# Moving the patch-projection tiles in the attention turns, and spreading the expert weight preparation over three units

## The reference

```python
h = patches(x) @ W + b                       # 768 -> 192 per token
a = layernorm(h)                             # attention, 12 heads of 16
q, k, v = heads(a @ Wq.T), heads(a @ Wk.T), heads(a @ Wv.T); rope(q), rope(k)
w = where(causal, erf(q @ k.T / 4) + 1, 0);  y = (w @ v) / max(sum(w), 1e-6)
h = h + y @ Wproj.T
n = layernorm(h)                             # mixture of experts
top-2 of 8 experts by softmax(n @ Wr), capacity 3920 tokens each, best weights first
routed = scatter_add(weight * (silu(d @ w1) * (d @ w3)) @ w2)     # inner width 768
shared = (silu(n @ s1) * (n @ s3)) @ s2
h = h + routed + shared
```

## Time and profile before

| | |
|---|---|
| median of three runs | 3525.04 us |
| profiled execution | 3521.11 us |
| its span | 3519.2 us |
| PE busy | 3201.1 us (91%) |
| DVE busy | 2435.4 us (69%) |
| ACT busy | 1557.7 us (44%) |
| POOL busy | 1389.7 us (39%) |
| mean granted PE clock | 0.914 of full |

### The profile page before, as it was taken

One profiled execution on the slowest core, in us unless ns is written; L12 is line 12 of the kernel. 1 busy time (PEld: TensorE's weight loads), 2 busy tenths in 40 slices (PEclk: granted clock), 3 DMA queues, 4 the chain that ended last, 5 costly groups with the idle time before them and its releaser, 6 DMA issues. The chain is left out here.

```text
span 3519.2 us, 71932 instructions
## 1 busy us (share of the span) xinstructions
PE 3201.1 (91%) x26164; PEld 2149.2 (61%) x26164; DVE 2435.4 (69%) x4832; ACT 1557.7 (44%) x3223; POOL 1389.7 (39%) x1170
## 2 busy tenths in 40 slices
PE   6999999999999999998229999989999999999997
PEld 5677667766776677666125555546565565555664
DVE  6998999999989998997655555554545445455443
ACT  2444445444544454443004444444445445444443
POOL 1222232223222322232205555036565565556664
PEclk9898889888988898885559999999999999999999
DMA  3232233333322333221111222134554445445443
GB/s 103 72 72 73 72 84 72 72 74 83 72 75 71 83 73 74 71 56 41 54 44 54 75 75 73 61 88 73 98 98 67 92 73 91 94 71 92 74 73 45
DMA packets 461610, 260.20 MB, mean 74 GB/s; under 512 B 339103, under 2 KB 442879, under 8 KB 457183
## 3 DMA queue, kind: packets, MB, share of 16 engines
q1 hardware_dynamic: 393632, 196.42, 23.2%
q0 software_dynamic: 54400, 49.00, 9.5%
q10 hardware_dynamic: 13262, 10.66, 0.9%
HBM read 107.98 MB, written 68.15 MB: 50 GB/s over the span
## 5 line engine op out<-in xcount | busy, mean ns | idle before, releaser
L1269 DVE SCALAR_TENSOR_TENSOR ffn_hidden<-ffn_up,ffn_silu 128x490 f32<-128x490 f32 (+2 forms) x534 | 350.6, 670 | 725.7 <-ACT ffn_silu L1250 630.7
L689 POOL TENSOR_TENSOR weights<-weights,x_pair 128x400 f32<-128x400 f32 x384 | 395.0, 1029 | 864.9 <-DVE weights L561 759.6
L1250 ACT ACTIVATE ffn_silu<-ffn_gate 128x490 f32<-128x490 f32 (+2 forms) x534 | 301.8, 582 | 746.3 <-PE ffn_up L1213 553.3
L1439 POOL DMA_INDIRECT out_rows<-done,ids x256 | 415.7, 1624 | 425.2 <-ACT done L1541 363.9
L1234 PE MATMUL ffn_out<-ffn_w_hi,ffn_hidden_hi 128*128 128x192 f16 (+1 forms) x2124 | 525.6, 247 | 15.9 <-ACT done L1541 11.9
L613 DVE RECIPROCAL recip<-x_product 128x200 f32<-128x200 f32 x384 | 534.3, 1391 | 0.0
L1235 PE MATMUL ffn_out<-ffn_w_lo,ffn_hidden_hi 128*128 128x192 f16 (+1 forms) x2124 | 522.8, 246 | 0.0
L1236 PE MATMUL ffn_out<-ffn_w_hi,ffn_hidden_lo 128*128 128x192 f16 (+1 forms) x2124 | 522.7, 246 | 0.0
L740 PE MATMUL bank<-w_qkv,normed_t 96*128 96x192 f32 (+1 forms) x1024 | 382.5, 535 | 44.3 <-ACT normed_t L411 44.3
L1244 ACT CAST ffn_hidden_hi<-ffn_hidden 128x490 f16<-128x490 f32 (+2 forms) x534 | 320.7, 601 | 105.2 <-DVE ffn_hidden L1269 103.3
L1262 DVE TENSOR_TENSOR ffn_hidden_lo<-ffn_hidden,ffn_hidden_hi 128x490 f16<-128x490 f32 (+2 forms) x534 | 356.1, 667 | 16.1
(11 more groups left out here) (176 smaller groups left out, 6932.3 us busy)
## 6 DMA issues: line engine op xcount, KB each, us to landing
patches<-in_patches SPq DMA_DIRECT2D x32, 1176.0 KB, 5.1
ffn_raw<-in_w SPq DMA_DIRECT2D x18, 768.0 KB
dram_x_t<-x_t SPq DMA_DIRECT2D x32, 392.0 KB, 3.4
x_t<-dram_x_t SPq DMA_DIRECT2D x24, 512.0 KB
base<-dram_h SPq DMA_DIRECT2D x24, 384.0 KB, 4.0
out_rows<-sums ACTq DMA_DIRECT2D x24, 384.0 KB, 4.7
v_held<-v SPq DMA_DIRECT2D x64, 102.0 KB, 2.3
dram_h<-h SPq DMA_DIRECT2D x32, 192.0 KB
```

Of the source, the lines that this page charges most:

```text
L689: nc.gpsimd.tensor_tensor(weights[:, n % 4], weights[:, n % 4], x_pair[:, n % 4, ::-1], ALU.mult)\
L1250: nc.scalar.activation(T.silu[:, m % 2, 0:n], T.gate[m % 2][:, 0:n], ACT.Silu, scale=1.0 / (TOKEN_SCALE * WEIGHT_SCALE)).then_inc(T.silued, 1)
L1269: nc.vector.scalar_tensor_tensor(T.hidden[:, m % 2, 0:n], T.up[m % 2][:, 0:n], HIDDEN_SCALE / (TOKEN_SCALE * WEIGHT_SCALE), T.silu[:, m % ...
L1439: nc.gpsimd.indirect_dma_start(out=dram["out"][:, :], out_offset=bass.IndirectOffsetOnAxis(ap=ids[i][0:height, t, 0:1], axis=0), in_=done[ ...
```

## The change

The token tiles get a bank each, and go to steps 2, 3, 7 and 8. The one of step 3 stands between the LN1T transposes and the wait for their copies. ACT copies each tile by itself (192 columns), ahead of whatever else it does in those steps. In the feed-forward part, the next expert's matrices are prepared one a unit, in units i = 1, 2 and 3.

```diff
 LN1T, QK, VV, YT, PROJ, X2T, ROUTE, TOK = (
-    (1, 2), (3, 4, 5, 6), (7, 10), (8, 9), (11, 12), (14, 15), (17,), (0, 13))
+    (1, 2), (4, 5, 6, 7), (8, 11), (9, 10), (12, 13), (16, 17), (19,), (0, 3, 14, 15))
...
 # ScalarE, after the copies of LN1T
+                    if n in (2, 3, 7, 8) and has_tokens:
+                        k = (2, 3, 7, 8).index(n)
+                        copy_out(TOK[k], h_new[slot][:, k, :], 128, D)
...
 # ScalarE, behind the copy of h in step 8
-                    if n in (1, 8) and has_tokens:
-                        k = n // 8
-                        copy_out(TOK[k], h_new[slot][:, 2 * k:2 * k + 2, :].rearrange("p t d -> p (t d)"), 128, 2 * D)
...
 # TensorE
                 def tokens(n):
-                    pos, at = TOK[n // 2], n % 2 * D
-                    out = room(pos) if n % 2 == 0 else bank[pos % NB]
+                    out = room(TOK[n])[:, 0:D]
                     for i in range(KP):
-                        last = nc.tensor.matmul(out[:, at:at + D], wide(patches[slot], i, n), tok_w[:, i, :],
+                        last = nc.tensor.matmul(out, wide(patches[slot], i, n), tok_w[:, i, :],
                                                 start=(i == 0), stop=(i == KP - 1))
-                    if n % 2:
-                        last.then_inc(full[pos % NB], 1)
+                    last.then_inc(full[TOK[n] % NB], 1)
...
                     if n == 3 and has_next:
                         pe.wait_ge(normed_ready, 4 * u + 8)
                         transposed(LN1T, normed)
+                    if n in (2, 3, 7, 8) and has_tokens:
+                        if n == 2:
+                            # the waits for patches_in that stood in step 0
+                        tokens((2, 3, 7, 8).index(n))
+                    if n == 3 and has_next:
                         copied(LN1T)
...
-                    if n in (0, 1, 7, 8) and has_tokens:
-                        # n == 0: the waits for patches_in
-                        tokens(n if n < 2 else n - 5)
...
 # the experts, ScalarE and VectorE
-                if i == 1 and not closing(e, i, 0):
+                if i in (1, 2, 3) and not closing(e, i, 0):
                     act.wait_ge(T.raw_in, 48 * e + 144)
-                    weights_hi(nc, T, 1 - ws)
+                    weights_hi(nc, T, 1 - ws, (i - 1,))
...
-                if i == 1 and not closing(e, i, 0):
-                    dve.wait_ge(T.weights_hi, 3 * e + 9)
-                    weights_lo(nc, T, 1 - ws)
+                if i in (1, 2, 3) and not closing(e, i, 0):
+                    dve.wait_ge(T.weights_hi, 3 * e + 6 + i)
+                    weights_lo(nc, T, 1 - ws, (i - 1,))
```

More of the change, by code:

```diff
@@ L770, in turn @@
                         transposed(LN1T, normed)
+                    if n in (2, 3, 7, 8) and has_tokens:
+                        if n == 2:
+                            if kind == "mid":
+                                pe.wait_ge(patches_in[slot], 16 * (prior + 3 - slot))
+                            else:
+                                pe.wait_ge(patches_in[slot], 16 * (u // 2 + 2))
+                        tokens((2, 3, 7, 8).index(n))
+                    if n == 3 and has_next:
                         copied(LN1T)
@@ L1151, in load_weights, with weights_hi, lower_parts, weights_lo @@
         sp.dma_start(dst[:], dram[src][bass.ds(e * 128, 128), :]).then_inc(T.raw_in, 16)
[L1154 to L1160, removed]
+def weights_hi(nc, T, ws, mats=(0, 1, 2)):
+    for n in mats:
+        nc.scalar.activation(T.w_hi[ws][n][:], T.raw[n][:], ACT.Copy, scale=WEIGHT_SCALE).then_inc(T.weights_hi, 1)
+def lower_parts(T, ws, mats=(0, 1, 2)):
     near, far, whole = slice(0, INNER), slice(INNER, 2 * INNER), slice(0, MI * D)
-    for n, parts in enumerate(((near, far), (near, far), (whole,))):
+    parts_of_mat = ((near, far), (near, far), (whole,))
+    for n in mats:
+        parts = parts_of_mat[n]
         for part in parts:
             yield T.raw[n][:, part], T.w_hi[ws][n][:, part], T.w_lo[ws][n][:, part], part is parts[-1]
-def weights_lo(nc, T, ws):
-    for raw, hi, lo, last in lower_parts(T, ws):
+def weights_lo(nc, T, ws, mats=(0, 1, 2)):
+    for raw, hi, lo, last in lower_parts(T, ws, mats):
         ins = nc.vector.scalar_tensor_tensor(lo, raw, WEIGHT_SCALE, hi, ALU.mult, ALU.subtract)
```

## The result

The changed kernel took 3431.72 us (median of four runs, 3427.70 to 3436.55) against 3522.47 us for the one before on the same chips: a ratio of 0.9744, 95% interval 0.9726 to 0.9763. It is 2.6% faster. The forecast was 3507 us, range 3472 to 3542: the sign was right, the size was not. The profiled execution took 3431.96 us.

A forecast was written before the change was run, and what follows sets the result against it. DVE and PE were each taken to pace half of an attention turn, PE to bound the experts. 3521.1 + 17 (attention) - 31 (expert idles) - 2 (experts' clock) = 3505 us, put as median 3507; range 3472 to 3542.

The forecast's parts named there:

- What bounds a turn: Attention loop: DVE paces residual add to transposes, 27.54 us, PE the rest, 21.38; 46.27 a turn without the 1.2 GHz stretch.
- Tile 0 free, tile 1 adds to PE's half: Attention steps 2 and 3: tile 0 hidden under DVE, cost 0; tile 1 net +1.78 us a turn, 48.05 at full clock.
- The clock: Attention, from step 3: 6.8 us at 1.2 GHz every turn, all on dense work; turns of 51.0 us, +17 us in total.
- rival A: Attention: tiles keep PE active enough and the clock no longer falls; turns of 48.05, -68 us, with experts 3420; chance 0.10.
- B: Step 3: 1.2 GHz stretch stays long in three of seven turns, starting on the tile; turns 52.5, 3549 us; chance 0.10.
- C: Attention: PE's extra 1.78 us is offset by fewer long low-clock stretches, turn stays 50.4; 3488 us; chance 0.22.
- D: Experts: idle stays, `put` or the split behind it being late in three units instead of one; 3538 us; chance 0.13.
- Expert weights: Experts, unit 1: both PE idles go, 4.37 us in seven experts, -31 us; clock falls behind two of them, -2 us.
- Copies, banks, queues at 0: Attention: new banks, two more ACT copies and work queued behind them; bounds 0 to +0.3 us a turn, taken as 0.

## Why the prediction was wrong, point by point

- **What bounds a turn**: right. DVE's half measured 25.89 us to the mask in both kernels, and PE's half held the rest. The turn at full clock was put 0.7 us too low for the kernel before, 46.27 where 46.93 was measured, since DVE bounds both halves then; for the change 48.05 was worked out and 47.92 measured.
- **Tile 0 free, tile 1 adds to PE's half**: right. The idle of 1.15 us before the mask of step 2 was there, and tile 1 added 2.06 us against the 2.15 taken, starting 3.80 us behind the mask where 3.86 (670.31 - 666.45) was worked out, as long as the clock had been up before it, and 4.22 in the turn shown.
- **The clock**: the step that failed. "I take 6.8 us in every turn", all of it on dense work, was right in the length and wrong in the place. I named the new idle time ahead of the mask of step 2 and let the clock fall only at or behind that of step 3. It fell at the first of them. The 6.8 us then lie on the mask wait, a weighted sum and tile 0; PE comes 1.45 us late to the transposes (1424.68 - 1421.58 = 3.10 behind the mask, against 1.65). ACT's copies, which PE would have waited for, are nearly ready by then: the lateness takes the place of most of the wait, 0.23 us instead of 1.25. The term was 2.95 us of lost clock a turn (51.0 - 48.05). It measured 0.4 in such a turn (48.34 - 47.92) and 1.7 in the seven with a stretch on tile 1 (49.60 - 47.92), on average 0.7 (48.64 - 47.92). Before, it was 3.5 (50.41 - 46.93), not the 4.1 taken. Hence 48.64 instead of 51.0, and 48 us gained instead of 17 lost. The time at 1.2 GHz also fell, from 10.1 to 6.1 us a turn, but that the forecast had (6.8), and it does not make the gain: with extra work in step 2 that time is 5.9 us, all of it in PE's half, and the turn is 50.25, nearly what it was before. That run and the one with tile 0 in step 0 (49.50) show that the place is what counts.
- **The rival A** (3420 us) came near in time, by a mechanism that did not happen, so its nearness is luck: the clock falls as often (30 times in 28 turns, 28 before), it is only cheaper. I gave it 0.10 since it needed the clock to hold. The Trainium skill, "TensorE: Matmul & The Clock Gate" (section "HAM oscillation — how this bites in real kernels"), was cited for it with its advice of dense work in place of waits. The extra products in step 3 agree with that (turns of 47.80 instead of 50.41 us), those in step 2 do not (50.25 instead of 48.64): there the fall went elsewhere and cost more.
- **The rivals B, C and D**: none came. Stretches of 13.6 us, on which B rested, are gone from the 28 turns; C's turn of 50.4 us did not come; and of D's idle time nothing is left.
- **Expert weights**: the mechanism was right, and all 31 us of idle time went. The clock's share was 8.5 of the 10 us of PE busy time, instead of 2; the experts gained 41 instead of 33. The forecast counted the stretches of 1.2 GHz behind two of the seven units, 7 us, and both went. It did not count those elsewhere, 17 us from 1860 us on, of which 10 went too; their number differs between kernels with the same experts. One sum was off: from ACT's start at 2640.97 to the end of DVE's work are 8.77 us, not 8.9; nothing hung on it.
- **Copies, banks, queues at 0**: right, 1.0004 in the run with the banks alone.

What stays open: why the clock falls at one idle time and not at another (seven of 28 turns of the changed kernel have a stretch on tile 1), why some of the falls that remain with six extra products move to another place, and why the number of falls in the experts differs. None was tested.

## What to carry to other kernels

When the clock falls once in each turn of a loop, ask in which half of the loop it falls: idle time ahead of a wait on the engine that paces, far from PE's dense work, was a cheap place for it here, and filling that idle time moved the fall to an expensive one. Filling the last idle time before the dense work is what paid, even with products that nobody reads, as long as they fit into the wait. A burst of side work on two engines that is longer than the slack of one unit costs its excess each time; split over units with the same slack it cost nothing here.

## What the runs showed of the hardware that was not expected

- More PE work made the kernel slower by moving the clock: three products of 1.24 us in all, inside an idle stretch of 1.15 to 1.4 us, cost 1.6 us a turn (48.64 to 50.25) at the same mean clock of 0.94.
- Six extra fp32 products of 192 columns, one ahead of the last mask wait and five behind the transposes, were enough to keep 2.4 GHz in 23 of 28 turns; a turn then is 46.94 us with PE's clock at 1.00.
- The clock can fall while PE is busy: at 565.9 in the kernel with six extra products PE had last idled 0.24 us.
- In the experts, removing 31 us of idle time shortened PE's busy time by 10 us for the same 11589 products.
